# Where the list pages of a mixture-of-experts kernel are padded: once behind the final counts, or page by page ahead of the rows

## The reference, cut to what matters

```python
x = x + xattn(layernorm(x), ctx, ctx, lens, Wq, Wk, Wv, Wo)
u = layernorm(x)
s = softmax(u @ centroids.T + expert_biases)
topk_vals, topk_idx = top_k(s, 2)
g_topk = sum(one_hot(topk_idx, 16) * topk_vals[..., None], axis=-2)
xe = einsum('bsd,eod->bseo', u, Wr) + br
routed = einsum('bse,bseo->bso', g_topk, xe)
shared = (einsum('bsd,eod->bso', u, Ws) + sum(bs, axis=0)) / 2
x = x + u + routed + shared
```

## Time and profile before

| | before |
|---|---|
| median of 3 runs | 261.77 us |
| profiled execution: device time | 261.29 us |
| its span in the trace | 259.4 us |
| its mean granted TensorE clock | 0.953 |
| busy: TensorE matmul | 219.6 us, 85% |
| busy: VectorE | 152.5 us, 59% |
| busy: GpSimd | 106.3 us, 41% |
| busy: ScalarE | 95.1 us, 37% |

### The profile page before, as it was taken

The page is one execution under the profiler, slowest core; times in us unless marked ns, Lnnn a source line. Parts: engine busy times, 40 slices in busy tenths (PEclk is TensorE's granted clock), DMA queues, the critical chain, the costliest instruction groups (busy, mean ns, idle before and its releaser), DMA issues.

```text
span 259.4 us, 5036 instructions
## 1 busy us (share of the span) xinstructions
PE 219.6 (85%) x1530; PEld 184.8 (71%) x1530; DVE 152.5 (59%) x457; ACT 95.1 (37%) x241; POOL 106.3 (41%) x176
## 2 busy tenths in 40 slices
PE   7888999999999999999997943988669978576593
PEld 3767888888899998888875832867547757454482
DVE  1798778888888888888645930657503313140460
ACT  3114567566656666555442001222202213110022
POOL 1220222444444555444667200467566566574000
PEclk9999999999999999999999995999995999997689
DMA  6999990101011111100212693667455541200997
GB/s 170 361 247 373 426 414 16 43 20 44 20 44 41 43 41 44 42 22 27 79 39 71 159 206 100 201 197 221 137 169 163 172 130 36 90 17 9 332 382 248
DMA packets 20345, 36.30 MB, mean 140 GB/s; under 512 B 4059, under 2 KB 12765, under 8 KB 19936
## 3 DMA queue, kind: packets, MB, share of 16 engines
q1 hardware_dynamic: 13568, 22.50, 27.4%
q0 software_dynamic: 3792, 8.42, 9.2%
q10 hardware_dynamic: 2960, 5.07, 6.5%
HBM read 23.23 MB, written 14.71 MB: 146 GB/s over the span
## 4 chain that ended last, share of the span: by engine, by line
PE 67%; issue 9%; DMA 8%; DVE 4%; another core or an unknown queue 3%; SPq 3%; POOL 3%; ACT 1%; ACTq 1%; DVEq 0%; POOLq 0%
PE O L886 13%; PE T L808 7%; PE B L845 6%; PE B L953 5%; PE S L808 5%; PE A L808 4%; PE S L857 4%; PE B L1057 4%; PE T L1057 4%; PE A L1057 3%; DMA x<-in_x 3%; PE O L1057 3%; SPq L321 2%; PE S L1076 2%
## 5 line engine op out<-in xcount | busy, mean ns | idle before, releaser
L537 POOL DMA_INDIRECT lists<-urow,pos x32 | 32.8, 1024 | 41.6 <-PE S L857 34.0
L488 ACT ACTIVATE uTl<-S 128x256 f32<-128x256 f32 x47 | 17.0, 383 | 58.5 <-PE S L808 37.1
L415 ACT ACTIVATE pT<-T 128x512 f32<-128x512 f32 (+1 forms) x48 | 25.2, 526 | 30.4 <-PE T L808 28.7
L886 PEld LDWEIGHTS O<-vfront,pT 128*128 128x128 f32 x256 | 30.0, 192 | 0.1
L886 PE MATMUL O<-vfront,pT 128*128 128x34 f32 x256 | 29.9, 273 | 0.0
L665 DVE TENSOR_REDUCE rowmax<-S 128x16 f32<-128x1232 f32 x16 | 23.1, 1442 | 7.2 <-PE S L857 7.1
L568 POOL DMA_INDIRECT y<-yrow,padblock x16 | 15.8, 989 | 27.9 <-DVE yrow L786 20.7
L808 PE MATMUL T<-const,s_sb 128*128 128x128 f32 (+1 forms) x160 | 25.4, 273 | 2.0 <-DVE s_sb L680 1.2
L808 PEld LDWEIGHTS T<-const,s_sb 128*128 128x128 f32 (+1 forms) x160 | 19.1, 139 | 4.5 <-issue 2.7
L441 ACT ACTIVATE urow<-x,shift,rstds 128x256 f32<-128x256 f32 x32 | 19.1, 596 | 8.4 <-POOL shift L551 7.5
L680 DVE SCALAR_TENSOR_TENSOR s_sb<-S,rstds,scaledmax 128x1024 f32<-128x1024 f32 (+1 forms) x26 | 21.0, 850 | 0.0
(11 more groups left out here) (188 smaller groups left out, 432.7 us busy)
## 6 DMA issues: line engine op xcount, KB each, us to landing
padblock<-lists SPq DMA_DIRECT2D x32, 128.5 KB, 1.7
wr<-in_wrT SPq DMA_DIRECT2D x1, 4096.0 KB, 17.8
br<-in_br SPq DMA_DIRECT2D x1, 2048.0 KB, 21.9
wr<-y SPq DMA_DIRECT2D x8, 256.0 KB, 7.2
wr<-y ACTq DMA_DIRECT2D x8, 256.0 KB, 8.2
urow<-lists SPq DMA_DIRECT2D x15, 128.5 KB
xT<-in_xT SPq DMA_DIRECT2D x3, 512.0 KB, 7.7
x<-in_x SPq DMA_DIRECT2D x3, 512.0 KB, 8.0
```

The source lines that it names most:

```text
L415: nc.scalar.activation(pT[t % 2][0:rows, c0:c1, :], T[0:rows, 0:c1 - c0, :], ACT.Exp).then_inc(p_ready, 1)
L537: nc.gpsimd.indirect_dma_start(out=lists, out_offset=bass.IndirectOffsetOnAxis(ap=pos[:, t, c:c + 1], axis=0), in_=urow[t % NR][c][:, :], ...
L886: last = M(to, pT[t % 2][0:v.shape[0], c, :], v.rearrange("p h j -> p (h j)"), start=(c == 0), stop=(c == CH - 1), skip_group_check=True)
```

## The change

The padding no longer waits for the final counts. At the start, GpSimd sets all 16 rows for each partition of `padblock`, and SP writes three pages of padding (384 rows) to each of the 16 regions, in three DMAs ahead of x, xT, `wr` and `br`; the last two groups of x tiles become one. During the loop, a third small matmul (`count_runs`) counts, on 128 partitions that stand for 16 experts by 8 runs of 16 rows, how far each list has grown before the tile. VectorE turns the count into a page number and a run number (`reached`, `page`, `dropped`, `run_i`), and one more indirect DMA for each of the tiles 1 to 13 writes the 128-row page that lies three tiles ahead; runs of lists whose page has not changed get a number outside and are dropped. `seen` becomes `seen_runs`, eight copies of each column. `pad_lists`, `padrow` and its table signal go. `HANDOVER` is 12 instead of 14.

```diff
-HANDOVER = 14
+HANDOVER = 12
+PARTS = P // EXPERTS
+RUN = P // PARTS
+REACH = 3
+BEYOND = 4096.0
+EIGHTS = 1.5 * 2.0 ** 26
...
-        seen = sb("seen", [P, EXPERTS], bf16)
+        seen_runs = sb("seen_runs", [P, EXPERTS, PARTS], bf16)
+        seen = seen_runs[:, :, 0]
...
-        XGROUPS = [(0, 2), (2, 4), (4, 8), (8, 12), (12, 16)]
+        XGROUPS = [(0, 2), (2, 4), (4, 8), (8, 16)]
...
-        def pad_lists(eng, engine, e0, e1):
...
-                    eng.dma_start(lists[ds(row, P), :].rearrange("(p r) w -> p (r w)", r=PIECE),
-                                  padblock[0:P // PIECE, 0:PIECE, :].rearrange("p r w -> p (r w)")).then_inc(padded, 16)
...
             sp.wait_ge(pool_set, 3)
-            sp.dma_start(lists[DUMMY:DUMMY + P, :], padblock[:, 0, :]).then_inc(padded, 16)
-            for g in (3, 4):
-                load_x(sp, g)
-                load_xT(sp, g)
+            sp.dma_start(lists[DUMMY:DUMMY + P, :], padblock[:, 0, :]).then_inc(filled, 16)
+            per_expert = lists[0:DUMMY, :].rearrange("(e n) w -> e n w", e=EXPERTS)
+            for page_of in range(REACH):
+                sp.dma_start(per_expert[:, page_of * P:(page_of + 1) * P, :].rearrange("e (b r) w -> e b (r w)", r=RUN),
+                             padblock[:, :, :].rearrange("p r w -> p (r w)")).then_inc(filled, 16)
+            load_x(sp, 3)
+            load_xT(sp, 3)
...
-            pad_lists(sp, mybir.EngineType.SP, 0, EXPERTS // 2)
-            sp.wait_ge(table_ready, 2)
+            sp.wait_ge(table_ready, 1)
...
-                    sp.wait_ge(padded, 16 + 16 * EXPERTS)
+                    sp.wait_ge(filled, 16 * (1 + REACH))
+                    for i in range(2):
+                        sp.wait_ge(padded[i], 16 * len(range(1 + i, TILES - REACH + 1, 2)))
...
-            pad_lists(act, mybir.EngineType.Activation, EXPERTS // 2, EXPERTS)
...
-            nc.gpsimd.memset(padblock[:, 0:PIECE, 0:D], 0.0)
-            nc.gpsimd.memset(padblock[:, 0:PIECE, D:ROW].bitcast(i32), PADROW).then_inc(pool_set, 1)
+            nc.gpsimd.memset(padblock[:, :, 0:D], 0.0)
+            nc.gpsimd.memset(padblock[:, :, D:ROW].bitcast(i32), PADROW).then_inc(pool_set, 1)
...
+                if t == 0:
+                    pool.wait_ge(filled, 16 * (1 + REACH))
+                if t >= REACH:
+                    pool.wait_ge(padded[(t - REACH) % 2], 16 * ((t - REACH) // 2 + 1))
...
+            def pad_page(t):
+
+                pool.wait_ge(run_ready, t)
+                nc.gpsimd.indirect_dma_start(
+                    out=runs, out_offset=bass.IndirectOffsetOnAxis(ap=run_i[:, t:t + 1], axis=0),
+                    in_=padblock[:, :, :].rearrange("p r w -> p (r w)"), in_offset=None,
+                    bounds_check=DUMMY // RUN - 1, oob_is_err=False).then_inc(padded[(t - 1) % 2], 16)
+
             for s in range(TILES + 3):
...
                     scatter_rows(s - 3, s)
+                if 1 <= s - 3 <= TILES - REACH:
+                    pad_page(s - 3)
...
                     dve.wait_ge(rank_psum, t + 1)
+                    opens = 1 <= t <= TILES - REACH
+                    if opens:
+                        V.tensor_scalar(reached[:, :], run_bank(t), REACH * P - FRONT - 0.5, 1.0 / RUN, ALU.add, ALU.mult
+                                        ).then_inc(reached_ready, 1)
...
-                        V.tensor_tensor(seen[:, :], seen[:, :], chosen[:, :], ALU.add)
+                        V.tensor_tensor(seen_runs[:, :, :], seen_runs[:, :, :],
+                                        chosen[:, :].unsqueeze(2).to_broadcast([P, EXPERTS, PARTS]), ALU.add)
...
                     V.scalar_tensor_tensor(out=pos[:, t, :], in0=idx8[:, 0:TOPK], scalar=float(REGION), in1=posf[:, :],
                                            op0=ALU.mult, op1=ALU.add).then_inc(pos_ready, 1)
+                    if opens:
+                        dve.wait_ge(reached_ready, t)
+                        link(V.tensor_scalar(page[:, t:t + 1], reached[:, :], EIGHTS, EIGHTS, ALU.add, ALU.subtract))
+                        link(V.tensor_scalar(dropped[:, :], page[:, t - 1:t], page[:, t:t + 1], BEYOND, ALU.is_equal, ALU.mult))
+                        V.scalar_tensor_tensor(out=run_i[:, t:t + 1], in0=page[:, t:t + 1], scalar=cst("run"), in1=dropped[:, :],
+                                               op0=ALU.add, op1=ALU.add).then_inc(run_ready, 1)
...
-            V.tensor_tensor(padrow[:, :], B[0:1, 0:EXPERTS], cst("region", 1), ALU.add).then_inc(table_ready, 1)
...
+            def count_runs(t):
+
+                if 1 <= t <= TILES - REACH:
+                    M(run_bank(t), seen_runs[:, :, :].rearrange("p e b -> p (e b)"), ones16[:, 0:1], start=True, stop=True)
...
+                    count_runs(t)
                     M(O[:, 0:EXPERTS], before16[:, :], chosen[:, :], start=True, stop=False)
```

More of the change, by code:

```diff
@@ L182, in build @@
         start_i = sb("start_i", [LISTS, 1], i32)
-        padrow = sb("padrow", [1, EXPERTS], i32)
-        RUN, PIECE, NL, NY, NU = 16, 4, 24, 16, 4
+        reached = sb("reached", [P, 1])
+        page = sb("page", [P, TILES])
+        dropped = sb("dropped", [P, 1])
+        run_i = sb("run_i", [P, TILES], i32)
+        NL, NY, NU = 24, 16, 4
         padblock = sb("padblock", [P, RUN, ROW])
@@ L193, in build @@
         part = sb("part", [P, 2, D])
-        warm = sb("warm", [P, 512])
+        warm = part[:, :, :].rearrange("p a d -> p (a d)")
         diag = [pT[c][:, 0:HALF, :] for c in range(TOPK)]
@@ L252, in build @@
         shifted_ready = sem("shifted_ready")
-        padded = sem("padded")
+        filled, padded, run_ready = sem("filled"), [sem(f"padded{i}") for i in range(2)], sem("run_ready")
+        reached_ready = sem("reached_ready")
         l_arrived = [sem(f"l_arrived{j}") for j in range(NL)]
@@ L310, in expert_column @@
                                   skip_runtime_bounds_check_because="the table keeps it at most the last expert")
-        def pad_lists(eng, engine, e0, e1):
-            eng.wait_ge(table_ready, 1)
-            eng.wait_ge(pool_set, 3)
-            for g in range(e0, e1, 4):
-                _, rows = nc.values_load_multi_w_load_instructions(
-                    padrow[0:1, g:g + 4], (engine,), min_val=0, max_val=DUMMY - P,
-                    skip_runtime_bounds_check_because="a list's end lies in its region")
-                for row in rows:
-                    eng.dma_start(lists[ds(row, P), :].rearrange("(p r) w -> p (r w)", r=PIECE),
-                                  padblock[0:P // PIECE, 0:PIECE, :].rearrange("p r w -> p (r w)")).then_inc(padded, 16)
         def list_load(eng, k, row):
@@ L505, in _ @@
             nc.gpsimd.memset(ones16[:, :], 1.0)
-            nc.gpsimd.memset(seen[:, :], 0.0).then_inc(pool_set, 1)
+            nc.gpsimd.memset(seen_runs[:, :, :], 0.0).then_inc(pool_set, 1)
             nc.gpsimd.memset(center[:, 1, :], -1.0 / D)
@@ L694, in take_shared @@
                                 x[:, 2 * i:2 * i + 2, :], ALU.add).then_inc(ws_taken, 2)
+            V.memset(page[:, 0:1], float((REACH - 1) * PARTS))
             dve.wait_ge(arrived["rest"], 16)
@@ L991, in rank @@
                     pe.wait_ge(rank_taken, t)
+                count_runs(t)
                 M(rank_bank(t), before16[:, :], chosen[:, :], start=True, stop=False)
-                M(rank_bank(t), ones16[:, :], seen[:, :], start=False, stop=True).then_inc(rank_psum, 1)
+                M(rank_bank(t), ones16[:, :], seen, start=False, stop=True).then_inc(rank_psum, 1)
             def route(t):
@@ L1031, in _ @@
             pe.wait_ge(out_taken, TILES)
-            M(B[:, 0:EXPERTS], ones16[:, :], seen[:, :], start=True, stop=False)
+            M(B[:, 0:EXPERTS], ones16[:, :], seen, start=True, stop=False)
             M(B[:, 0:EXPERTS], ones16[:, :], chosen[:, :], start=False, stop=True).then_inc(count_psum, 1)
```

13 lines of the change are left out of this document (8 added, 5 removed).

## The result

In the comparison made for the prediction, the changed kernel takes 267.87 us (median of 4 runs, 264.09 to 359.74) and the kernel before 261.10 (4 runs, 259.94 to 262.01). The ratio rests on the two fast runs of the changed kernel (264.09 and 266.49) and leaves out two slow ones, 359.74 (at a mean granted clock of 0.547) and 269.25, which is the execution that was profiled: **1.0167, interval 1.0116 to 1.0217**. The change makes the kernel some 4 us slower, 1.7%. 263.2 was forecast, inside 259.5 to 267.5; 1.0167 times 261.1 is 265.5.

What follows compares the result with a forecast made beforehand. The prediction took TensorE and VectorE together to bound the loop, and the padding's landing the list stage. 7.7 (VectorE) + 1.3 (GpSimd) + 2.8 (start) - 10.4 (removed) = +1.4 us, forecasting 263.2, range 259.5 to 267.5.

Steps and rivals of the forecast that it cites:

- a slower clock: Rival at the start: TensorE's longer wait drops its clock, the first tile costs about 2 us more; 265.2, chance 0.2.
- long rows on GpSimd: Rival: the page's indirect DMA with 16 KB rows takes 3.3 us or more on GpSimd; 267.7, chance 0.12.
- the step of 8.0: Sign in the loop: TensorE's queries start about 0.7 later, directly behind VectorE's addition, in a step of about 8.0 us.
- the gap ahead of the list stage: Sign behind the loop: TensorE goes from shared experts to list transposes with a gap under 1 us, no half clock.
- the first scaled maximum: Sign at the start: VectorE's first scaling instruction, beside the memset, takes about 3.5 us.
- the start: Term at the kernel's start: the longer memset on GpSimd holds VectorE's first scaling instruction until it ends, adding 2.8 us.
- the removed wait: Term behind the loop: without the final padding, the list stage starts at 150.7 in place of 159.6, gaining 8.9 us.
- the clock behind it: Term at the list stage: with the gap gone TensorE's clock stays up, gaining 1.5 us on transposes and first matmuls.
- VectorE in the loop: Term: instructions ahead of the residual addition cost 0.70 us a tile, 7.7 us together.
- The rival that these additions hide: Rival in the loop: the addition has slack, so VectorE's 7.7 us shrink to about 1; 256.5, chance 0.12.
- GpSimd: the price: Term: one more indirect DMA a tile takes 1.26 us, hidden in the loop; behind it, tile 12's page costs 1.3.
- There is time: At the start: SP's 6.3 MB fill delays nothing, as x tiles, first scatter and weights are wanted later.

Runs made afterwards that it cites:

- e0_again: The changed kernel once more, unedited: 266.28 us, 1.0116 of the kernel before.
- e1_memset_waits: The changed kernel, with GpSimd's memset of padblock started only behind VectorE's first scaled maximum: 265.63 us, 1.0129 of the kernel before.
- e4_pool_order: The changed kernel, with GpSimd behind the loop scaling tile 15 first and issuing tile 13's page ahead of tile 13's scatter: 267.14 us, 1.0206 of the kernel before.
- f1_reach4: The changed kernel with four pages filled at the start and pages written for tiles 1 to 12 only: 253.41 us, 1.0144 of the kernel before.
- f2_spread: The changed kernel with a page's runs dealt over the partitions expert by expert, so one expert's packets come from partitions 16 apart: 251.54 us, 1.0102 of the kernel before.
- f3_before_memset: The kernel before, with only the memset of padblock enlarged to 16 rows a partition from 4: 254.36 us, 1.0216 of the kernel before.
- h3_late_weights: h1_three with four pages ahead and the routed experts' weight and bias loads held back to mid-loop: 265.53 us, 1.0176 of the kernel before.
- h1_three: The changed kernel with the memset delayed, page, dropped and run_i behind the top 2, and runs dealt expert by expert: 260.44 us, 0.9966 of the kernel before.
- i_pieces: h1_three with weights and biases in six 1 MB loads, each behind the landing of one of the first six pages: 241.74 us, 0.9702 of the kernel before.

## Why the prediction was right or wrong

The range held and the signs of all four terms were right; the likeliest class was not. I gave 0.44 to a time within 1% and 0.38 to slower by over 1%, and it is slower by 1.7%. The working adds up to +1.4; the ratio gives +4.4, and the profiled execution, itself outside the range, +8.0. That the range held is in part luck: its upper end was there for a slower clock and for long rows on GpSimd, while the largest of the four misses had no share in it. Of the signs that I had named, the step of 8.0 came; the gap ahead of the list stage (3.84 us, not under 1, at half clock) and the first scaled maximum (2.41, not 3.5) did not. The 6.6 us between +1.4 and the trace's +8.0 lie in the start (4.45 in place of 2.8), the loop (8.2 in place of 7.0), the removed wait (3.9 in place of 6.9) and the clock behind it (0.8 in place of 1.5).

**VectorE in the loop: right.** 0.70 a tile was forecast, 0.65 is measured from scaled maximum to addition, and the step grows from 7.34 to 8.00. Its order, with `posf` covered by `placed` and each linked neighbour some 0.2 apart, is what the timeline shows. Over the loop behind tile 5 this makes ten steps of 0.66, 6.6 of the 8.2. The rival that these additions hide is dead: 0.63 us of idle TensorE stand in each step. The rest, 1.6, is a half clock inside the loop, which no step of mine had. It follows once TensorE stands idle in each step, in this execution and in those of e0_again, e1_memset_waits and e4_pool_order; in f1_reach4 and f2_spread, with the same idle time, it does not come. It comes and goes between executions, and what decides it stays open.

**The start: mechanism right, sizes wrong.** VectorE was held to the end of the memset, as read from one meeting of 0.70 us, and e1_memset_waits undoes it. The hold was priced too high: the instruction takes 2.41 us (2.58 in f3_before_memset), 1.7 to 1.9 more than its 0.70 before, and not 2.8 more, since the memset takes 3.50 and not 3.8 and starts nearer to the score maximum. But the clock fell too, and the rest of the 4.45 at tile 5, some 2.7, comes with it: in e0_again, where the half clock is 3.4 us shorter, tile 5 is reached 1.6 us earlier. I had that as a rival of its own, with 0.2 and 2 us, beside the forecast. That 2.8 + 2 = 4.8 is close to the 4.9 of f3_before_memset is two errors that cancel. The half clock belonged into the forecast: in the trace of the kernel before it begins within the gaps of TensorE of 7.7 us at 151.9, of 3.1 at 192.0 and of 4.6 at 238.0. It did not have to come (a gap of 3.4 us at 113.5 in h3_late_weights has none), but 0.2 was low for it.
The Trainium skill, page "SBUF — State Buffer", section "Who interferes with whom", says that VectorE's copies and `tensor_scalar` can take two ports and then block against GpSimd for a whole instruction. The trace of e1_memset_waits agrees for both kinds of instruction: beside the same memset, the small COPY at 15.82 takes 1.96 and ends with it, and the SCALAR_TENSOR_TENSOR at 14.28, a form that the section does not list as one that takes two ports, takes 1.62, as it does elsewhere.

**GpSimd: the price right, what hangs on it not quite.** The page DMA takes 1.00 us of GpSimd, with rows of 16 KB as a scatter with rows of 1 KB (0.96), and in the loop it is hidden. Behind the loop the page of tile 12 delays the scale of tile 15, as forecast, and with it more than GpSimd: TensorE stands 1.97 us, to 154.36, for the row that is made from it, which the forecast lacks. In e4_pool_order, where the scale goes first, this wait is gone. It is covered by the wait for the last scatter here, and not in f1_reach4. The rival of long rows was wrong about the engine. It was right that long rows cost something, in another place: their packets.

**The removed wait: the failed step.** The prediction said: "The page of tile 13 is issued two scatters ahead of the end and writes few pages, so I give this no share of its own." The diff has the line that refutes it: the scatter of tile t waits for `padded` of tile t - 2, so the scatter of tile 15 waits for the page of tile 13. I had counted how long the page would keep GpSimd's queue and not when it would land. It takes 4.6 to 7.1 us, where the last scatter behind it takes 2.4 to 2.6, and the scatter of tile 15 stands 1.5 to 4.0 us for it. Few pages do not help, since one expert's eight packets go two at a time, in four waves. The list stage came 3.9 us nearer, in place of 8.9 - 0.7 - 1.3 = 6.9 (5.2 in e0_again, where the page landed sooner), and the gap of 3.8 us that is left brought the half clock back, so that behind it 0.8 was gained in place of 1.5. f2_spread and f1_reach4 take the page out of the chain in two ways, and the first list matmuls then run at full clock. In f2_spread the list stage comes 38.86 - 31.96 = 6.9 us nearer, which is the forecast's own number (within it, the last scatter lands in 2.43 us and not 3.0, and is issued 2.5 us later behind tile 15 where 2.0 were forecast). f1_reach4, at 1.0144, shows the next bound: TensorE's shared work, late by start, loop and the row of tile 15.

**What was costed at nothing.** The two shared tiles moved to the end cost nothing, as said: from the first load of returned rows to the end it is 20.8 before and 20.6 after. The filling also cost nothing that the trace of the changed kernel shows: tile 5 is reached at 51.8 with it and at 52.6 in f3_before_memset without it. Its cover was thin, though: the pages go out some 5 us later there than in the repaired kernel. "There is time" was true for x and the first scatter and not for the page of tile 1, which h1_three shows.

**What stays open.** The kernel before differs by 11 us between groups of runs. The chip is not what differs: the third and the fourth group ran on the same one. In the slower groups the chain of waits has one to three stops of 3.5 to 5 us in the list stage, under "another core or an unknown queue", at which ACT and VectorE wait together; in the faster ones none is in the chain. No edit of mine touched them, their cause stays open, and they are why only ratios within a group are used. i_pieces was measured in a group without the stops, so that its 3.0% is shown for that case alone.

## What to carry to other kernels

Before a wait is moved off the end, write down which of the last instructions waits for which landing, and price the landing, not the issue: here the last scatter stood 1.5 to 4.0 us for a page, and in the profile after 3.0 us of the gain went with it. An instruction in front of the one that feeds the bound engine costs its full length in each step; three such instructions, moved half a step later, gave back 0.58 of the 0.66 us. Bulk writes that are free while the loop is late can stand in the way of small ones once it is on time; here they were split, and each piece was tied to a landing.

## What the runs showed of the hardware

- A memset of 128x4096 on GpSimd (3.50 us) held a VectorE TENSOR_SCALAR of 16 elements a partition for 2.41 us and a COPY of the same size for 1.96, and left a SCALAR_TENSOR_TENSOR of 1024 elements at its 1.62.
- An indirect DMA costs GpSimd 0.96 us with rows of 1 KB and 1.00 with rows of 16 KB. What grows is the landing: packets of 16,448 bytes take 0.61 us each against 0.16 to 0.19 for the row scatter's records of 4,112, and those of neighbouring partitions go one behind another. The page of tile 13 lands in 4.6 to 7.1 us in this order, and in 3.4 in f2_spread and i_pieces. Its last large packet had ended at 158.96 in the profile after, 2 us ahead of the landing; packets of the row scatters issued behind it run in these 2 us (159.93 to 160.99), and whether the landing waits for them is open.
- A dropped run is still a packet, of 4 bytes and 7 to 9 ns.
- Beside the queue of filling, x and weights, the same indirect DMA landed 15.9 us behind its issue in h1_three, where the median of i_pieces is 4.3.
